# Mixing and 16-head attention of a four-block decoder as one program block on one Trainium2 core

## The chip, the cores and the metric

The kernel runs on one core of one Trainium2 chip. The metric is the device time of one execution in microseconds; the kernel before was run three times (1469.81, 1473.39 and 1476.22 us, median 1473.39). One further execution was recorded by the hardware profiler; that one took 1470.31 us, of which 1468.5 us lie between its first and its last instruction. The instruction queues are called by their engines: TensorE (PE, with its weight loads PEld), VectorE (DVE), ScalarE (ACT), GpSimd (POOL) and SyncE (SP, which issues the DMAs).

## The reference

The input x has 32 sequences of 128 tokens with 128 features (float32). Four layers alternate cross attention against a context (128 tokens, 96 features) and a feed-forward part, each added to x. What matters here is the end of layer 1 and the start of layer 2:

- layer 1's block takes the result of its first attention, modulated, adds a state-space convolution, runs a multilayer part `gelu(LN(z) W1 + b1) W2 + b2`, normalises and adds it to x;
- layer 1's feed-forward part picks one of 8 experts **per sequence**: each expert's small autoencoder (128 to 32 and back) tries to reconstruct the normalised tokens, the expert with the least error wins, and its down and up matrices (128 to 64 to 128, with relu) are added to a shared product with W_base, gated;
- layer 2's attention has 16 heads of 8 features: q from LN(x), k and v from the context, softmax over the 128 context tokens, an output matrix Wo with bias, gated and added to x. Layer 2's feed-forward part quantises LN(x) with one scale for the whole tensor, so it needs the largest absolute value of all of it.

## The kernel before, in words

X stays in on-chip memory (`k.X`, 128 partitions of tokens, 32 sequences). The stages run one after the other, each a block of programs for the five queues, with a barrier and a clearing of its semaphores behind it (class OneTime, the clear and barrier are reported at L72): `stage_front`, `stage_film`, `stage_mix` (L1679), `stage_attention16` (L2096), `stage_last`. The two in the middle are the ones touched.

**stage_mix** works on groups of four sequences (8 groups) in a software pipeline, loop variable n from -1 to 10, written out by hand in the same order for all queues. In step n group n goes through the multilayer part (L1857, L1828, L1902), group n-1 is normalised, added to X and normalised again to `xa` (L2013, third use), group n-2 goes through the reconstruction (transposes of xa L1862, L1832, L1843, L1845, the squares L2066, the loss L2069, the four small products L1922 to L1925, then the gain and the choice `at`, L2089 to L2093), and for group n-3 SyncE loads the four chosen numbers into registers (L1758) and issues four DMAs for the down matrices (L1765) and four for the up matrices (L1770); TensorE waits for them and does the down products (L1888), ScalarE the relu (L1994), TensorE the output products (L1913, L1915), VectorE adds them to X (L2084). In TensorE's queue the output products of group n-3 stand before the small sums of group n-2. Steps 8, 9 and 10 are the last three: there is no multilayer part left in them, and in step 10 only the last group's expert. GpSimd computes reciprocal square roots (L1783, L1785) and some sums of whole groups; its last work is in step 8.

**stage_attention16** prepares constants (GpSimd: zeroes v, top, sel, L2169 to L2173; VectorE: mod32, hmask, nsel, bo, L2335 to L2345, with one product on TensorE, L2204) and then runs a pipeline over n from -7 to 37. Steps below 0 open it: for group 0 statistics (L97), moments (L178 to L188), rstd (L2179), application (L195), then one item per step on PSUM bank 7, k (L2275), x transposed (L2279), q (L2283) and v (L2286), each evacuated by ScalarE. GpSimd adds the bias to X (L2189) and masks q for the four bands of heads (L2197). From then on each n is a sequence: scores (L2219), peak of each row (L2351), its transpose (L2258), scores transposed with the peak subtracted (L2231, L2235), exp (L2299), product with v (L2249) and sums (L2253), reciprocal, Wo (L2266), sum into X (L2399). The next group's k, x, q and v are made one per step beside it. The scores of sequence 0 belong to step n = -1. The last stage begins with the largest value (L2724).

The waits are counters; each queue runs its instructions in the order in which they are written, so an instruction that waits holds up all behind it in its queue.

Of the kernel before, what the change touches and what calls it, by code (L numbers as in the profile page):

```python
# [5 lines left out]
F32 = mybir.dt.float32  # L6
# [1672 lines left out]
def stage_mix(nc, w, ps, k):  # L1679
# [5 lines left out]
    GROUPS = B // G  # L1685
    with ExitStack() as ctx:
# [3 lines left out]
        fo, u_ = tmp("fo", [128, 2, G, 256]), tmp("u", [128, 3, G, 128])  # L1690
        z, last = tmp("z", [128, 3, G, 128]), tmp("last", [128, G, 128])
        nmr = tmp("nmr", [128, B])
        xn, hT = tmp("xn", [128, G, 128]), tmp("hT", [128, W])
        hid = tmp("hid", [128, 4, W])
# [3 lines left out]
        xa, xaT = tmp("xa", [128, G, 128]), tmp("xaT", [128, 2, W])  # L1698
# [24 lines left out]
        ve1_done, ve2_done, ve3_done = (once(n) for n in ("ve1_done", "ve2_done", "ve3_done"))  # L1723
        block = ctx.enter_context(nc.Block())
# [17 lines left out]
        def flat(ap):  # L1742
            return ap.rearrange("p j d -> p (j d)")

# [68 lines left out]

        @block.tensor
        def _(pe):
# [34 lines left out]

            for n in range(FIRST, LAST):
# [26 lines left out]
                if has(n - 2):  # L1878
                    recon(n - 2, 1)
                if has(n - 3):  # L1880
# [24 lines left out]
                if has(n - 3):  # L1905
# [10 lines left out]
                    m.then_inc(out_ps, 1)  # L1916
                if has(n - 2):
# [7 lines left out]
                    pe.matmul(o, k.ones[:, 0:G], k.bd2q[:], start=False, stop=True).then_inc(sum_ps, 1)  # L1925

        @block.scalar
        def _(act):
# [30 lines left out]

            plain(0)  # L1960
            for n in range(FIRST, LAST):
# [24 lines left out]
                if has(n + 2):  # L1986
                    plain(n + 2)
                if has(n - 3):
# [4 lines left out]
                    for j in range(G):  # L1993
                        act.activation(aT[0:R, j, :], ps[0:R, 0, j * S:j * S + S], ACT.Relu,  # L1994
                                       bias=dn[0:R, g % 2, j, R:R + 1]).then_inc(aT_done, 1)

        @block.vector
        def _(dve):
# [11 lines left out]
            def apply(dst, src, mv, rs, rs_done, done, g):  # L2010
                dve.wait_ge(rs_done, g + 1)
                for j in range(G):
                    dve.tensor_scalar(dst[:, j, :], src[:, j, :], mv[:, j, 0:1], rs[:, j:j + 1], ALU.subtract,  # L2013
                                      ALU.mult).then_inc(done, 1)

            for n in range(FIRST, LAST):
# [69 lines left out]
                if has(n - 2):  # L2086
# [6 lines left out]
                    dve.max_index(at[:], best[:], gain[:]).then_inc(at_done, 1)  # L2093


def stage_attention16(nc, w, ps, k):  # L2096

    H, DH = 16, 8
    SCALE = DH ** -0.5
    R = 4
    GROUPS = B // G
    with ExitStack() as ctx:
        def tmp(name, shape, dt=F32):
            return ctx.enter_context(nc.sbuf_tensor("g_" + name, shape, dt))

        nm = Norm(lambda n, s: ctx.enter_context(nc.sbuf_tensor(n, s, F32)), "g")  # L2110
        on = Norm(lambda n, s: ctx.enter_context(nc.sbuf_tensor(n, s, F32)), "go")
        xall = k.x3[:].rearrange("p a b -> p (a b)").rearrange("p (b c) -> p b c", b=B)
        xn, xnT = tmp("xn", [128, 2, G, 128]), tmp("xnT", [128, W])
        qT, kT = tmp("qT", [128, 2, W]), tmp("kT", [128, 2, W])
        mod32, hmask = tmp("mod32", [128, 32]), tmp("hmask", [128, R])
        nsel = tmp("nsel", [128, R, 128])
        mq = tmp("mq", [128, 3, R, 128])
        v, sel = tmp("v", [128, 2, G, R, 160]), tmp("sel", [128, 160])
# [992 lines left out]
```

## Time and profile before

| | |
|---|---|
| runs, median (lowest to highest) | 1473.39 us (1469.81 to 1476.22) |
| profiled execution, its span | 1470.31 us, 1468.5 us |
| instructions | 30801 |
| TensorE busy, mean granted clock | 1182.5 us (81%), 0.862 |
| VectorE, ScalarE, GpSimd busy | 997.4, 689.2, 545.7 us |
| mixing, 16-head attention (first to last instruction) | 492.4 to 695.9, 697.0 to 938.7 us |

Times in a timeline are microseconds from the first instruction. A row of it is a run of like instructions on one queue: start, length from the first start to the last end, engine, line, operation, tiles written and read, shape, count; in brackets the idle time of the engine in front of it and what ended that. [...]

### The profile page before, as it was taken

Reading aid. Unit: us, or ns where it says so; the run is one execution under the profiler, and the core shown is the slowest. Engines: PE = TensorE matmul, PEld = TensorE weight load, DVE = VectorE, ACT = ScalarE, POOL = GpSimd, SP = SyncE. Lnnn points to the kernel's source line nnn. Section 1 sums busy time; section 2 is a strip of 40 time slices with the busy share of each in tenths; the row PEclk is TensorE's granted clock in tenths of the full one; section 3 lists DMA queues with packets and bytes.
Section 4 is the critical chain, followed back from the end, with each engine's and each line's share of the span. In section 5 each row is a group of like instructions: output and inputs, shape, how many; then the busy total and the mean of one; then the engine's idle time right before and its main releaser. Section 6 shows DMA issues by size and latency. Waiting matters only on the chain. (4 is left out here: it accounts for less than half of the span.)

```text
span 1468.5 us, 30801 instructions
## 1 busy us (share of the span) xinstructions
PE 1182.5 (81%) x10551; PEld 809.7 (55%) x10551; DVE 997.4 (68%) x3895; ACT 689.2 (47%) x2022; POOL 545.7 (37%) x769
## 2 busy tenths in 40 slices
PE   4767764667766678885699988589999989999998
PEld 3533322434444455553477777356666657777766
DVE  6767759999996478851577776677776654544443
ACT  3343336777764334321244544347666653433333
POOL 4576565777664255520322231244333320000000
PEclk7779775776766699995799999789999999998989
DMA  6301031010002411000000000000000000000000
GB/s 167 95 1 33 12 99 47 16 30 19 26 23 73 122 29 44 16 15 15 2 3 3 3 3 3 1 1 1 2 1 1 2 1 1 15 0 14 0 15 15
DMA packets 63745, 35.59 MB, mean 24 GB/s; under 512 B 23989, under 2 KB 61488, under 8 KB 63602
## 3 DMA queue, kind: packets, MB, share of 16 engines
q1 hardware_dynamic: 62298, 33.45, 8.3%
q8 instruction: 79, 1.29, 0.4%
q14 instruction: 64, 0.52, 0.1%
q10 hardware_dynamic: 1304, 0.33, 0.1%
HBM read 25.21 MB, written 6.42 MB: 22 GB/s over the span
## 5 line engine op out<-in xcount | busy, mean ns | idle before, releaser
L2994 DVE SCALAR_TENSOR_TENSOR k_X<-ps,m_gt,k_X 128x128 f32 (+1 forms) x256 | 72.2, 345 | 120.9 <-PE ps L2878 120.8
L2917 ACT ACTIVATE m_hid<-ps,k_b 128x512 f32<-128x512 f32 x128 | 81.8, 684 | 133.2 <-PE ps L2878 127.7
L2878 PEld LDWEIGHTS ps<-k_w,m_hid 128*128 128x128 f32 x1024 | 123.1, 192 | 26.8 <-issue 19.6
L2867 PE MATMUL ps<-m_xnT,k_w 128*128 128x512 f32 x256 | 128.2, 631 | 1.3 <-PEq L72 1.3
L2878 PE MATMUL ps<-k_w,m_hid 128*128 128x128 f32 x1024 | 123.4, 275 | 0.0
L2538 POOL TENSOR_TENSOR l_p<-l_p,l_rsum 128x512 f32<-128x512 f32 x64 | 65.2, 1039 | 139.2 <-DVE l_rsum L2816 139.2
L2351 DVE TENSOR_REDUCE g_top<-ps 128x8 f32<-128x1024 f32 x64 | 75.4, 1220 | 50.4 <-PE ps L2219 50.4
L1587 DVE MATCH_REPLACE8 v_left<-c_top,v_left 128x128 f32<-128x128 f32 x384 | 107.2, 410 | 0.0
L2299 ACT ACTIVATE g_pT<-ps 128x1024 f32<-128x1024 f32 x64 | 62.0, 1021 | 85.3 <-PE ps L2235 85.3
L2670 ACT ACTIVATE l_p<-ps,l_shift 128x128 f32<-128x128 f32 x256 | 91.4, 389 | 21.2 <-DVE l_shift L2757 19.9
L711 PE MATMUL ps<-f_expT,f_xeT 128*128 128x512 f32 x128 | 73.3, 705 | 27.4 <-DVE k_X L1089 27.3
L1581 DVE MAX8 c_top<-v_left 128x8 f32<-128x128 f32 x384 | 84.0, 403 | 0.0
L1587 DVE MATCH_VALUE_LOAD v_left<-c_top,v_left 128x8 f32 x384 | 73.7, 214 | 0.0
L121 POOL TENSOR_TENSOR m_rstd<-m_ve,k_half 128x8 f32<-128x8 f32 x4 | 6.6, 1639 | 175.0 <-DVE m_ve L114 175.0
L2867 PEld LDWEIGHTS ps<-m_xnT,k_w 128*128 128x128 f32 x256 | 47.8, 205 | 41.2 <-issue 41.2
L842 ACT ACTIVATE f_part<-ps,f_wf 128x128 f32<-128x128 f32 x128 | 36.4, 368 | 72.6 <-issue 47.0
L1389 PE MATMUL ps<-k_ident,c_exa 128*128 128x128 f32 x256 | 56.4, 411 | 10.4 <-POOL c_exa L1334 10.4
L1389 PEld LDWEIGHTS ps<-k_ident,c_exa 128*128 128x128 f32 x256 | 53.9, 318 | 18.3 <-POOL c_exa L1334 18.1
L711 PEld LDWEIGHTS ps<-f_expT,f_xeT 128*128 128x128 f32 x128 | 25.5, 223 | 65.9 <-DVE k_X L1089 44.9
L2670 ACT ACTIVATION_READ_ACCUMULATOR l_p<-ps,l_shift 128x1 f32 x256 | 58.8, 230 | 0.0
L1089 DVE SCALAR_TENSOR_TENSOR k_X<-ps,f_wf,k_X 128x128 f32<-128x128 f32 x128 | 44.6, 349 | 20.3 <-PE ps L711 16.3
L1373 PE MATMUL ps<-c_kT,c_qT 32*128 32x128 f32 x256 | 21.7, 419 | 45.3 <-ACT v_sc L1468 42.6
(537 smaller groups left out, 3178.2 us busy)
## 6 DMA issues: line engine op xcount, KB each, us to landing
v_toep<-kpad SPq DMA_DIRECT2D x4, 1024.0 KB, 9.3
fo_dram<-c_fo SPq DMA_DIRECT2D x32, 128.0 KB
d_fo<-fo_dram SPq DMA_DIRECT2D x8, 512.0 KB, 3.6
k_X<-in_x SPq DMA_DIRECT2D x8, 256.0 KB, 3.5
v_late<-kpad SPq DMA_DIRECT2D x2, 1024.0 KB, 8.4
out<-k_X SPq DMA_DIRECT2D x8, 256.0 KB, 2.4
f_cx<-in_ctx SPq DMA_DIRECT2D x4, 384.0 KB, 5.5
c_cx<-in_ctx SPq DMA_DIRECT2D x4, 384.0 KB, 4.3
```

Of the source, the lines that this page charges most:

```text
L711: pe.matmul(ps[:, 4 + (2 * b + h) % 3, :], xeT[:, t % 2, u, cols], expT[:, 4 * h:4 * h + 4, :].rearrange("p e d -> p (e d)"), start=True, ...
L1389: m = pe.matmul(ps[:, 4 + a, 0:128], exa[:, i % 4, h, :], k.ident[:], start=h == 0, stop=h == H - 1)
L1581: dve.max((first if r == 0 else top)[:, a, h, :], (sc if r == 0 else left)[:, i % 4, h, :]).then_inc(top_done, 1)
L1587: dve.match_replace(left[:, i % 4, h, :], (first if r == 0 else top)[:, a, h, :], (sc if r == 0 else left)[:, i % 4, h, :], TAKEN).then_in ...
L2299: act.activation(pT[:, n % 2, 2 * h:2 * h + 2, :].rearrange("p a n -> p (a n)"), ps[:, 4 + 2 * h:6 + 2 * h, :].rearrange("p a n -> p (a n) ...
L2351: dve.tensor_reduce(top[:, (n + 1) % 2, :].rearrange("p (r c) -> p r c", r=R)[:, 2 * h:2 * h + 2, 0:R], ps[:, 2 * h:2 * h + 2, :].rearrang ...
L2538: pool.tensor_tensor(p[:, n % 3, 4 * a:4 * a + 4, :], p[:, n % 3, 4 * a:4 * a + 4, :], rsum[:, n % 3, 4 * a:4 * a + 4].rearrange("p (h o) ...
L2670: act.activation(p[:, i % 3, h, :], ps[:, 2 * (i % 2) + a, 128 * b:128 * b + 128], ACT.Exp, bias=shift[:, i % 2, h:h + 1], scale=SCALE, ac ...
L2867: pe.matmul(ps[:, 4 * u + q, :], k.w1_3[:, e, 128 * q:128 * q + 128], xnT[:, u], start=True, stop=True).then_inc(s["hid_ps"].sem, 1)
L2878: m = pe.matmul(ps[:, 4 * u + 2 + e % 2, j * S:j * S + S], hid[:, u, q, j * S:j * S + S], k.w2_3[:, e, q, :], start=q == 0, stop=q == 1)
L2917: act.activation(hid[:, u, q, :], ps[:, 4 * u + q, :], ACT.Gelu, bias=k.b1_3[:, 2 * e + q:2 * e + q + 1]).then_inc(s["hid"].sem, 1)
L2994: dve.scalar_tensor_tensor(out=xj[u][j], in0=ps[:, 4 * u + 2 + e % 2, j * S:j * S + S], scalar=gt[:, u, j, e:e + 1], in1=xj[u][j], op0=ALU ...
```

## The change

The two stages become one, `stage_mix_attend`, with one block. The attention's step becomes a function `attend(n)` on each queue, called with the old bodies. Names that clashed are renamed (xn to an, xnT to anT, top to peak, topT to peakT, out_ps to ao_ps, x_done to sum_done, R to BANDS). The bias product goes to PSUM bank 2 instead of 0. Eight of the mixing's tiles no longer have memory of their own: they are parts of the attention's v and pT, so that zeroing v waits until the last multilayer product is made and the last z begun.

Where the opening steps are called now, in the mixing's last three steps (GROUPS is 8, so GROUPS + 1 is step 9). The memory:

```diff
+        v, pT = keep("v", [128, 2, G, BANDS, 160]), keep("pT", [128, 2, BANDS, W])
+        low = v[:].rearrange("p u j a x -> p (u j a x)")
+        fo = low[:, 0:2048].rearrange("p (u j c) -> p u j c", u=2, j=G)
+        hid = low[:, 2048:4096].rearrange("p (q n) -> p q n", q=4)
+        xn = low[:, 4096:4608].rearrange("p (j d) -> p j d", j=G)
+        hT = low[:, 4608:5120]
+        low = pT[:].rearrange("p u a n -> p (u a n)")
+        u_ = low[:, 0:1536].rearrange("p (u j d) -> p u j d", u=3, j=G)
+        z = low[:, 1536:3072].rearrange("p (u j d) -> p u j d", u=3, j=G)
+        last = low[:, 3072:3584].rearrange("p (j d) -> p j d", j=G)
+        xa = low[:, 3584:4096].rearrange("p (j d) -> p j d", j=G)
```

GpSimd, behind the mixing's whole loop:

```diff
+            pool.wait_ge(mlp_ps, GROUPS)
+            pool.wait_ge(zs, GROUPS)
+            pool.memset(v[:], 0.0).then_inc(zeroed, 1)
+            pool.memset(peak[:], 0.0).then_inc(zeroed, 1)
+            pool.memset(sel[:], 0.0).then_inc(zeroed, 1)
+            pool.wait_ge(zeroed, 3)
+            pool.memset(sel[:].rearrange("p (b x) -> p b x", x=40)[:, :, 0:DH], 1.0).then_inc(sel_done, 1)
...
+            for n in range(OPEN, CLOSE):
+                attend(n)
```

TensorE, in the mixing's loop and behind it:

```diff
                 if has(n - 2):
                     recon(n - 2, 1)
+                if n == GROUPS + 1:
+                    pe.matmul(ps[:, 2, 0:128], k.bv2[:].broadcast_to([128, 128]), k.wo2[:], start=True,
+                              stop=True).then_inc(bvo_ps, 1)
+                    pe.wait_ge(left, GROUPS)
+                    attend(-5)
+                if n == GROUPS + 2:
+                    attend(-2)
                 if has(n - 3):
                     g = n - 3
...
                     m.then_inc(out_ps, 1)
+                if n == GROUPS + 1:
+                    attend(-4)
                 if has(n - 2):
...
                     pe.matmul(o, k.ones[:, 0:G], k.bd2q[:], start=False, stop=True).then_inc(sum_ps, 1)
+                if n == GROUPS + 1:
+                    attend(-3)
+
+            pe.wait_ge(bo_sum, 1)
+            pe.wait_ge(sel_done, 1)
+            pe.wait_ge(nsel_done, 1)
+            attend(-1)
+
+            pe.wait_ge(gain_done, GROUPS)
+            pe.wait_ge(xo_done, GROUPS)
+            for n in range(0, CLOSE):
+                attend(n)
```

ScalarE:

```diff
                 if has(n + 2):
                     plain(n + 2)
+                if n == GROUPS + 1:
+                    attend(-5)
+                if n == GROUPS + 2:
+                    act.wait_ge(zeroed, 3)
+                    attend(-3)
+                    attend(-2)
                 if has(n - 3):
...
+                if n == GROUPS + 1:
+                    attend(-4)
+
+            for n in range(-1, CLOSE):
+                attend(n)
```

VectorE (the four places are behind sx, behind the loss, behind xa and at the end of the step):

```diff
                     dve.tensor_reduce(sx[:], xaT[:, g % 2, :].rearrange("p (j t) -> p j t", j=G), AX.X,
                                       ALU.add).then_inc(sx_done, 1)
+                if n == GROUPS + 1:
+                    attend(-5)
...
+                if n == GROUPS + 1:
+                    dve.tensor_reduce(mod32[:], k.ident[:].rearrange("p (r c) -> p c r", r=BANDS), AX.X,
+                                      ALU.add).then_inc(mod_done, 1)
+                    dve.wait_ge(mod_done, 1)
+                    dve.tensor_reduce(hmask[:], mod32[:].rearrange("p (b d) -> p b d", b=BANDS), AX.X,
+                                      ALU.add).then_inc(hmask_done, 1)
+                    dve.wait_ge(bvo_ps, 1)
+                    dve.tensor_tensor(bo[:], ps[:, 2, 0:128], k.bo2[:], ALU.add).then_inc(bo_sum, 1)
+                    dve.wait_ge(bo_sum, 1)
+                    dve.tensor_scalar(bo[:], bo[:], k.tg[:, 2:3], None, ALU.mult).then_inc(bo_done, 1)
...
                     apply(xa, group(k.X, g), mv3, rs3, rs3_done, xa_done, g)
+                if n == GROUPS:
+                    attend(-7)
+                    attend(-6)
...
                     dve.max_index(at[:], best[:], gain[:]).then_inc(at_done, 1)
+                if n == GROUPS + 1:
+                    dve.tensor_scalar(nsel[:], mod32[:, 0:BANDS].rearrange("p (b o) -> p b o", o=1).broadcast_to([128, BANDS, 128]),
+                                      -1.0, None, ALU.mult).then_inc(nsel_done, 1)
+                    dve.wait_ge(zeroed, 3)
+                    attend(-3)
+                    attend(-2)
+
+            for n in range(-1, CLOSE):
+                attend(n)
```

And the list of stages:

```diff
-        stages = [stage_front, stage_film, stage_mix, stage_attention16, stage_last]
+        stages = [stage_front, stage_film, stage_mix_attend, stage_last]
```

What `attend` does at the steps named: on VectorE -7 the statistics and -6 the moments of group 0, -5 its application to `an`, -3 and -2 statistics and moments of group 1, -1 the peaks of sequence 0; on TensorE and ScalarE -5 k, -4 x, -3 q, -2 v of group 0, -1 the scores of sequence 0 and k of group 1. On GpSimd -6 is rstd of group 0, -4 the bias into X of group 0, -2 rstd of group 1 and then the masked q of sequence 0, -1 that of sequence 1.

## Rows read from the trace of the kernel before

**Rows 1.** The page: span of the profiled execution.
```profile
span 1468.5 us, 30801 instructions
```

**Rows 2.** Busy by stretch: us, PE, PEld, DVE, ACT, POOL, granted clock, DMA, GB/s.
```profile
661.40:678.00 16.60, 13.54 (x54) 8.24 (x50) 4.64 (x10) 3.09 (x7) 0.00 (x0) 0.71 0.07 17
678.00:697.00 19.00, 5.92 (x30) 5.17 (x26) 1.81 (x7) 1.12 (x4) 0.04 (x1) 0.50 0.06 14
697.00:714.90 17.90, 9.89 (x50) 5.72 (x50) 9.83 (x31) 2.57 (x4) 10.46 (x9) 0.51 0.01 1
```

**Rows 3.** Timeline, the mixing's last step (10).
```profile
678.98 0.15 DVE L2093 FIND_INDEX8 d_at<-d_best,d_gain 4x8 uint32<-4x8 f32 x1
...
689.32 1.94 PE L1888 MATMUL ps<-d_xaT,d_dn 128*64 128x128 f32 x8 [11.21 <-DMA d_up<-k_wup]
...
694.49 0.63 PE L1915 MATMUL ps<-d_up,d_aT 65*128 65x128 f32 x2
695.16 0.75 DVE L2084 SCALAR_TENSOR_TENSOR k_X<-ps,k_tg,k_X 128x512 f32<-128x512 f32 x1 [16.04 <-PE ps L1915]
```

**Rows 4.** Timeline, the attention's opening up to the first peak.
```profile
696.96 4.36 POOL L2169 MEMSET g_v<- 128x5120 f32 x1 [41.44 <-POOLq L72]
...
697.51 4.10 DVE L2340 TENSOR_SCALAR g_nsel<-g_mod 128x512 f32<-128x512 f32 x1
...
702.05 0.87 DVE L97 BATCH_NORM_STATS2 g_stats<-k_X 128x6 f32<-128x128 f32 x4
702.08 0.12 POOL L2173 MEMSET g_sel<- 128x32 f32 x1
...
702.30 2.04 PE L2275 MATMUL ps<-k_cT,k_wk 96*128 96x512 f32 x2 [4.54 <-POOL g_sel L2173]
...
703.71 0.17 DVE L188 TENSOR_SCALAR g_ve<-g_m 128x4 f32<-128x4 f32 x1
...
706.26 1.09 PE L2279 MATMUL ps<-k_ident,g_xn 128*128 128x128 f32 x4 [1.91 <-DVE g_xn L195]
...
712.95 1.95 PE L2219 MATMUL ps<-g_kT,g_mq 32*128 32x128 f32 x32
...
714.97 2.35 DVE L2351 TENSOR_REDUCE g_top<-ps 128x8 f32<-128x1024 f32 x2 [6.75 <-PE ps L2219]
```

**Rows 5.** Timeline, end of the mixing's step 8 on GpSimd and VectorE.
```profile
654.48 1.04 POOL L1785 TENSOR_TENSOR d_rs<-d_rs,k_half 128x4 f32<-128x4 f32 x1
...
656.55 1.11 DVE L2013 TENSOR_SCALAR d_xa<-k_X,d_mv,d_rs 128x128 f32<-128x128 f32 x4
...
661.31 0.75 DVE L2084 SCALAR_TENSOR_TENSOR k_X<-ps,k_tg,k_X 128x512 f32<-128x512 f32 x1 [3.65 <-PE ps L1915]
...
662.42 0.15 DVE L2093 FIND_INDEX8 d_at<-d_best,d_gain 4x8 uint32<-4x8 f32 x1
```

**Rows 6.** Timeline, the mixing's step 9.
```profile
661.48 1.12 PE L1862 MATMUL ps<-k_ident,d_xa 128*128 128x128 f32 x4
...
672.82 1.15 PE L1888 MATMUL ps<-d_xaT,d_dn 128*64 128x128 f32 x8 [2.37 <-DMA d_up<-k_wup]
...
677.92 0.20 PE L1925 MATMUL ps<-k_bd2q,k_ones 128*4 128x8 f32 x2
678.54 0.14 DVE L2089 TENSOR_SCALAR d_gain<-ps 4x8 f32<-4x8 f32 x1
```

**Rows 7.** First VectorE instruction behind the seam into mixing and into attention.
```profile
492.48 0.19 DVE L1999 TENSOR_TENSOR d_nmr<-k_mv,k_rstd 128x32 f32<-128x32 f32 x1 [1.16 <-PEq L72]
...
697.00 0.37 DVE L2335 TENSOR_REDUCE g_mod<-k_ident 128x32 f32<-128x128 f32 x1 [1.08 <-PEq L72]
```

**Rows 8.** Timeline, one output product of step 7.
```profile
642.76 0.39 PE L1915 MATMUL ps<-d_up,d_aT 65*128 65x128 f32 x2
```

**Rows 9.** Timeline, scores of the third and the fourth sequence.
```profile
725.37 1.17 PE L2219 MATMUL ps<-g_kT,g_mq 32*128 32x128 f32 x32 [0.52 <-ACT g_topT L2304]
...
731.67 1.17 PE L2219 MATMUL ps<-g_kT,g_mq 32*128 32x128 f32 x32 [0.38 <-DVE g_oT L2394]
```

More of the change, by code:

```diff
@@ L1676, in _, with stage_mix_attend @@
                 dve.tensor_copy(chunk(c), ps[:, c, :])
-def stage_mix(nc, w, ps, k):
+def stage_mix_attend(nc, w, ps, k):
     R, E = 64, 8
     GROUPS = B // G
+    H, DH = 16, 8
+    SCALE = DH ** -0.5
+    BANDS = 4
     with ExitStack() as ctx:
@@ new lines, in stage_mix_attend @@
+        nsel = keep("nsel", [128, BANDS, 128])
+        mq = keep("mq", [128, 3, BANDS, 128])
+        sel = keep("sel", [128, 160])
+        peak, peakT = keep("peak", [128, 2, 128]), keep("peakT", [128, 2, 128])
+        rsum, oT = keep("rsum", [128, 128]), keep("oT", [128, 2, 128])
+        bo = keep("bo", [128, 128])
+        each = ctx.enter_context(OneTime(nc, "g_"))
+        zeroed, sel_done, mod_done, hmask_done, nsel_done, bvo_ps, bo_sum, bo_done = (
+            each(n) for n in ("zeroed", "sel_done", "mod_done", "hmask_done", "nsel_done", "bvo_ps", "bo_sum",
+                              "bo_done"))
@@ new lines, in stage_mix_attend @@
+        stats, halves, square, mean, ve, rstd, an_done, xb = (
+            each(n) for n in ("stats", "halves", "square", "mean", "ve", "rstd", "an_done", "xb"))
+        o_stats, o_halves, o_square, o_mean, o_ve, o_rstd, o_shift, o_done, most_done = (
+            each(n) for n in ("o_stats", "o_halves", "o_square", "o_mean", "o_ve", "o_rstd", "o_shift", "o_done",
+                              "most_done"))
+        onorm = dict(stats=Signal(o_stats, 0, 2 * G, k.apart), halves=Signal(o_halves, 0, 6, k.apart),
+                     square=Signal(o_square, 0, 4, k.apart), mean=Signal(o_mean, 0, 2, k.apart),
+                     ve=Signal(o_ve, 0, 2, k.apart))
@@ new lines, in stage_mix_attend @@
+        k_ps, kT_done, xT_ps, xT_done, q_ps, qT_done, v_ps, v_done = (
+            each(n) for n in ("k_ps", "kT_done", "xT_ps", "xT_done", "q_ps", "qT_done", "v_ps", "v_done"))
+        mq_done, sc_ps, top_done, topT_ps, topT_done, st_ps, ex_done, av_ps, rsum_done, oT_done, ao_ps, sum_done = (
+            each(n) for n in ("mq_done", "sc_ps", "top_done", "topT_ps", "topT_done", "st_ps", "ex_done", "av_ps",
+                              "rsum_done", "oT_done", "ao_ps", "sum_done"))
+        norm = dict(stats=Signal(stats, 0, 2 * G, k.apart), halves=Signal(halves, 0, 6, k.apart),
+                    square=Signal(square, 0, 4, k.apart), mean=Signal(mean, 0, 2, k.apart),
+                    ve=Signal(ve, 0, 2, k.apart), rstd=Signal(rstd, 0, 2, k.apart),
+                    xn=Signal(an_done, 0, 2 * G, k.apart))
@@ L1743, in flat, with item, evacuated, batch @@
             return ap.rearrange("p j d -> p (j d)")
+        OPEN, CLOSE = -7, B + 6
+        def item(n):
+            g, what = (n + 5) // G, ("k", "x", "q", "v")[(n + 5) % G]
+            return (what, g) if n >= -5 and g < GROUPS else (None, g)
+        def evacuated(eng, n):
+            what, g = item(n)
+            if what == "k":
+                eng.wait_ge(kT_done, g + 1)
+            elif what == "x":
+                eng.wait_ge(xT_done, g + 1)
+            elif what == "q":
+                eng.wait_ge(qT_done, g + 1)
+            elif what == "v":
+                eng.wait_ge(v_done, g + 1)
+        def batch(n):
+            return (n // G) % 2, slice((n % G) * S, (n % G) * S + S)
         @block.sync
```

499 lines of the change are left out of this document (207 added, 292 removed).

## The prediction

> **What bounds the kernel now.** I first read the page for the whole [rows 1]: 1468.5 us of span inside a profiled execution of 1470.31 us, which is 3.08 us under the median of the three runs (1473.39). [...]
>
> The timeline gives the chains. Last mixing step [rows 3]: the expert is chosen at 679.1, SyncE loads the four numbers and issues eight DMAs, TensorE waits 11.21 us and starts L1888 only at 689.32 when the last `up` has landed, then the output matmuls to 695.12 and the sum into X at 695.16. All engines are nearly free from 679 to 689. Opening of the attention [rows 4]: a barrier, a memset of v (4.36 us), then statistics, transposes, q, v, masked q, and at 712.95 the first scores; the first peak reduction starts at 714.97. From L2204 to 712.95 nothing is overlapped with mixing. What is moved ends in front of the scores, and all that follows them waits for them, so the number to find is when the scores of batch 0 start.
>
> **The change, part by part.**
>
> *Removed from the seam.* Scores start at 712.95, the last L1915 of mixing ends at 694.49 + 0.63 = 695.12 [rows 3, 4]. In the changed order of TensorE nothing stands between the two but waits for constants, v and masked q. If these are long done, scores follow at once: **-17.8 us** (712.95 - 695.12). The barrier is in it.
>
> *Are they done?* What is left after the step-9 sums (steps are numbered as the loop's n; 8, 9, 10 are the last three) is in the trace the way from the transposes L2279 (706.26) to the scores (712.95), 6.7 us [rows 4], at the low clock too. It starts at about 678 and so ends near 685, plus 2 to 3 us for nsel and the statistics of group 1, behind which POOL's masking waits: 688 at the latest, against TensorE's own 695. Cover: the 11.21 us of DMA wait. Some 7 us to spare, so I cost all of k, x, q, v, masking, nsel at nothing. Without that cover it would be the 6.7.
>
> *The memsets, step 8.* They sit behind POOL's last mixing work, which ends at 654.48 + 1.04 = 655.52 [rows 5]. In the trace they last from 696.96 to 702.20, 5.24 us [rows 4], so to about 660.8. VectorE wants to start `xa` (L2013, four tensor_scalar, 1.11 us) at 656.55 [rows 5], inside the big memset. The row for that: nsel, a tensor_scalar begun at 697.51 beside the same memset, took 4.10 us and ended 0.3 after it [rows 4], where four of a quarter of its size take 1.11 [rows 5]. So xa ends near 655.55 + 4.36 + 1.11 = 661.0 instead of 657.66. The transposes of xa start at 661.48 anyway [rows 6]: free. But behind xa the change puts the statistics and moments of group 0, 702.05 to 703.88 = 1.83 us [rows 4], to 662.9; the sum into X, due at 661.31 [rows 5], is 1.6 late, and the choice of expert at 662.57 with it. From there the chain (SyncE, DMA, L1888) runs without slack. **+1.6.** Bounds: 0, if the memset doesn't block (3.65 us of idle time before 661.31 take 1.83), and 3.0 if each small memset also stops one of the four. I take the middle one, as the row is of the same pair of instructions. [...]
>
> *Step 9.* The k matmul and the bias product go into TensorE's wait for the DMA, the gap before L1888, 2.37 us in this step [rows 6] and 1.6 longer with the delay above; k takes 2.04 at the low clock [rows 4], the other is a quarter as wide: free. On VectorE the application for group 0 (1.1) comes before the work that waits for L1845, and the constants (1.2) after the loss, both well ahead of the sum into X and the gain at 678.54 [rows 6]. The transposes of x do fall in the chain: they stand between the output matmuls and the four sums. They cost 1.12 at low clock, by the four at L1862 of the same form [rows 6]. The sums end at 677.92 + 0.20 = 678.12, the gain is taken at 678.54 [rows 6], so 0.4 is free: **+0.7** (0.2 if the clock is high; at most 1.1).
>
> *Step 10.* On SyncE's queue nothing is added. ScalarE's evacuations of q and v stand in front of aT, VectorE's nsel, statistics and moments in front of the sum into X; both have the DMA wait as cover. 0.
>
> *The end.* Two sets of semaphores are now cleared together at the end of the attention, where one was cleared at each seam. The seam with one set shows 1.08 us of idle time, the seam into mixing, which clears two, 1.16 [rows 7]. **+0.1** (up to 1.1, a whole seam).
>
> *Shared memory.* The waits that guard it (last multilayer product, last z) are long past where they are used, and the mixing loop keeps its own waits: 0. Steps 0 to 7 should be unchanged.
>
> Sum: -17.8 + 1.6 + 0.7 + 0.1 = **-15.4 us**. Against the profiled execution 1470.3 - 15.4 = 1454.9; against the median 1473.39 - 15.4 = **1458.0**, which I give.
>
> **Rivals.**
>
> *A, the delays don't come (gain 17 to 19.5).* The memset blocks nothing (+1.6 more), the transposes hide (+0.7), and TensorE's clock stays high in step 9: at 642.76 the two passes of a product at L1915 take 0.39 us, at low clock 0.63 [rows 3, 8]; over the eight products of the output phase that is 1.9 us. For it: the idle time before L1888 in step 9 is partly filled. Against: 1.6 us of new idle time. [...] Time 1454 to 1456.
>
> *B, the chain takes more (gain 10 to 13).* If all added VectorE and TensorE work of steps 8 and 9 falls into the chain of choosing: 3.0 + 1.1 + 1.2 + 1.1 instead of 2.3, 4.1 less: 1462. For it: that chain has no slack. Against: the idle times named.
>
> *C, the preparation isn't ready (gain 5 to 9).* One of its eight hand-overs waits behind a mixing instruction until after the DMA, and the rest, up to 6.7, follows it: 1464.7. Against it: each is issued before the dn matmuls.
>
> [...]
>
> **How the numbers follow.** Forecast 0.55; A 0.24, B 0.11, C 0.05, D 0.03, and 0.02 that the seam hides something that gives back most of it. 0.5% is 7.4 us, about what a measurement of this kernel can tell from no change. Forecast, A and B are faster by more (0.90), and so is a part of C: 0.92; the rest of C and the hidden thing: 0.05; D: 0.03. Range: from A's best with the lowest run before (1469.8 - 19 = 1451) to B's with some spread above, 1464.
>
> **What would show it.** In the changed profile: memset of v from about 655.5, the xa group at some 4 us instead of 1.11, the sum into X of step 8 at 663; choice of step 9 1.6 us, L1888 of step 10 about 2.3 us later than 689.32; scores of batch 0 right after the last L1915, near 697.4; first peak reduction near 699.4 instead of 714.97; the same 6.3 us per batch; one seam of about 1.2 us in front of the last stage. Wrong would be: scores that wait for a masked q or v, mixing steps 0 to 7 of another length, or a granted clock under 1.0 past the third batch.

## The result and the profile after

The changed kernel took **1456.38 us** (median of five runs, 1452.09 to 1462.50), the kernel before beside it 1473.39 us (five runs, 1469.81 to 1476.22): a ratio of 0.9888, 95% interval [0.9856, 0.9919], so 17.0 us less. The range (1451 to 1464) held it, and the forecast of 1458.0 was 1.6 us too high. The same kernel, run again unedited, gave 1457.35 us against 1472.81 (ratio 0.9893 [0.9876, 0.9910], 15.5 us less).

The execution that was profiled is the fastest of its five. The page's first line, to set beside [rows 1]:

```profile
span 1450.3 us, 30794 instructions
```

18.2 us less than before, but not all of it is the change's. The timeline at the start of mixing, whose code is the old one:

```profile
487.64 0.19 DVE L2266 TENSOR_TENSOR d_nmr<-k_mv,k_rstd 128x32 f32<-128x32 f32 x1 [1.16 <-PEq L72]
```

In [rows 7] it stands at 492.48; when the changed kernel was run again, unedited, it stood at 494.36. The stages ahead of mixing vary by 6.7 us between executions of the same instructions, so I compare profiles from this instruction on: to the first reduction of the last stage it is 447.23 us before (939.71 - 492.48) and 433.71 after (921.35 - 487.64), **13.5 us less**.

**Step 8.** The timeline of GpSimd and VectorE, which answers [rows 5]:

```profile
650.79 4.37 POOL L1891 MEMSET g_v<- 128x5120 f32 x1
651.86 4.36 DVE L2280 TENSOR_SCALAR g_pT<-k_X,d_mv,d_rs 128x128 f32<-128x128 f32 x4
...
656.15 0.63 PE L2117 MATMUL ps<-d_up,d_aT 65*128 65x128 f32 x2
...
657.85 0.74 DVE L2422 SCALAR_TENSOR_TENSOR k_X<-ps,k_tg,k_X 128x512 f32<-128x512 f32 x1
...
658.96 0.15 DVE L2431 FIND_INDEX8 d_at<-d_best,d_gain 4x8 uint32<-4x8 f32 x1
```

`xa` (its tile is now part of pT) takes 4.36 us instead of 1.11: one of its four pieces alone is shown as 3.79 us long, and the memset beside it ends at 655.16. The last output product ends at 656.78 and the sum into X starts 1.07 us behind it, where it started 0.04 behind before (660.64 + 0.63 against 661.31). The choice is 1.03 late.

**Step 9**, the timeline of all engines, which answers [rows 6]:

```profile
665.82 1.02 PE L2030 MATMUL ps<-k_cT,k_wk 96*128 96x512 f32 x2
...
669.35 1.94 PE L2090 MATMUL ps<-d_xaT,d_dn 128*64 128x128 f32 x8 [2.50 <-DMA d_up<-k_wup]
...
674.52 0.63 PE L2117 MATMUL ps<-d_up,d_aT 65*128 65x128 f32 x2
...
674.95 0.92 PE L2034 MATMUL ps<-k_ident,g_an 128*128 128x128 f32 x4
...
676.18 0.15 DVE L2427 TENSOR_SCALAR d_gain<-ps 4x8 f32<-4x8 f32 x1 [0.24 <-PE ps L2129]
...
676.64 0.15 DVE L2431 FIND_INDEX8 d_at<-d_best,d_gain 4x8 uint32<-4x8 f32 x1
```

k (one float32 product, which its row counts as x2; in front of it the bias product, 0.39) lies in the wait for the DMA. The transposes of x (L2034) stand between outputs and sums: the gain comes 1.03 behind the last output product (675.15), before 0.71 (677.83 to 678.54). From the first down product to the end of the outputs it is 5.80 us, before 5.01: the down products took 1.94 us at a granted clock of 0.50, before 1.15 at 0.86. I call 0.50 the lower level and 1.00 the high one: the first scores of this profile, below, took 2.09 us at 0.50 and the third 1.17 at 1.00.

**The preparation, step 10 and the seam that is gone** (timeline, answering [rows 3, 4]):

```profile
676.65 1.10 PE L2038 MATMUL ps<-g_anT,k_wq 128*128 128x512 f32 x2 [0.50 <-ACT g_anT L2196]
...
679.91 2.04 POOL L1919 TENSOR_TENSOR g_mq<-g_qT,g_hmask 128x512 f32<-128x512 f32 x2
680.34 0.60 ACT L2206 ACTIVATE g_v<-ps 128x512 f32<-128x512 f32 x1 [1.81 <-PE ps L2041]
...
686.97 1.94 PE L2090 MATMUL ps<-d_xaT,d_dn 128*64 128x128 f32 x8 [6.67 <-DMA d_up<-k_wup]
...
692.14 0.64 PE L2117 MATMUL ps<-d_up,d_aT 65*128 65x128 f32 x2
692.71 2.09 PE L1974 MATMUL ps<-g_kT,g_mq 32*128 32x128 f32 x32
692.82 0.75 DVE L2422 SCALAR_TENSOR_TENSOR k_X<-ps,k_tg,k_X 128x512 f32<-128x512 f32 x1 [13.98 <-PE ps L2117]
694.87 2.36 DVE L2287 TENSOR_REDUCE g_peak<-ps 128x8 f32<-128x1024 f32 x2 [1.30 <-PE ps L1974]
...
699.39 2.09 PE L1974 MATMUL ps<-g_kT,g_mq 32*128 32x128 f32 x32
...
706.33 1.17 PE L1974 MATMUL ps<-g_kT,g_mq 32*128 32x128 f32 x32 [0.52 <-ACT g_peakT L2187]
```

All of group 0 is ready at 681.95, 10.8 us before the scores, and these follow the last output product at once. From the choice to the down products it is 10.33 us, before 10.34. The third scores are at the high level (1.17 us, 1.00), as they were, and the fourth start 6.30 us behind them (712.63), as in [rows 9].

**The end.** The first row of the last stage, first of the kernel before (not shown above), then of the changed kernel:

```profile
939.71 0.16 DVE L2724 TENSOR_REDUCE l_amax<-k_most 128x1 f32<-128x8 f32 x1 [1.03 <-PEq L72]
```

```profile
921.35 0.16 DVE L2764 TENSOR_REDUCE l_amax<-k_most 128x1 f32<-128x8 f32 x1 [1.78 <-PEq L72]
```

0.75 us more for two clearings in a row.

### The profile page after: what moved, and what is told of

Read it like the earlier page. It is cut to its first block and busy times, and to the rows that moved or that the text cites. A ratio compares the mean times of both kernels' runs of the same rounds, so it can differ in the third digit from the quotient of the medians.

```text
span 1450.3 us, 30794 instructions
## 1 busy us (share of the span) xinstructions
PE 1175.4 (81%) x10551; PEld 805.8 (56%) x10551; DVE 995.7 (69%) x3895; ACT 689.0 (48%) x2022; POOL 545.8 (38%) x769
## 5 line engine op out<-in xcount | busy, mean ns | idle before, releaser
L2287 DVE TENSOR_REDUCE g_peak<-ps 128x8 f32<-128x1024 f32 x64 | 75.4, 1219 | 45.8 <-PE ps L1974 45.8
L1587 DVE MATCH_REPLACE8 v_left<-c_top,v_left 128x128 f32<-128x128 f32 x384 | 100.8, 274 | 0.0
L1581 DVE MAX8 c_top<-v_left 128x8 f32<-128x128 f32 x384 | 77.8, 274 | 0.0
L1389 PE MATMUL ps<-k_ident,c_exa 128*128 128x128 f32 x256 | 55.9, 407 | 10.3 <-POOL c_exa L1334 10.2
L1389 PEld LDWEIGHTS ps<-k_ident,c_exa 128*128 128x128 f32 x256 | 53.5, 316 | 18.1 <-POOL c_exa L1334 17.9
L1452 ACT ACTIVATE c_exb<-v_left,c_shift 128x128 f32<-128x128 f32 x128 | 49.6, 391 | 12.9 <-DVE v_left L1587 12.9
```

Source lines behind the costliest of these rows:

```text
L1389: m = pe.matmul(ps[:, 4 + a, 0:128], exa[:, i % 4, h, :], k.ident[:], start=h == 0, stop=h == H - 1)
L1581: dve.max((first if r == 0 else top)[:, a, h, :], (sc if r == 0 else left)[:, i % 4, h, :]).then_inc(top_done, 1)
L1587: dve.match_replace(left[:, i % 4, h, :], (first if r == 0 else top)[:, a, h, :], (sc if r == 0 else left)[:, i % 4, h, :], TAKEN).then_in ...
L2287: dve.tensor_reduce(peak[:, (n + 1) % 2, :].rearrange("p (r c) -> p r c", r=BANDS)[:, 2 * h:2 * h + 2, 0:BANDS], ps[:, 2 * h:2 * h + 2, :] ...
```

## The experiments

All kernels compute the reference, and each ran beside the kernel before, to which its ratio refers. The kernels of a group below ran on one chip; there the kernel before took 1472.81 us in the first group, 1472.78 in the second and 1471.52 in the third.

### First group: is it the overlap, and are the terms there?

**The changed kernel again, no edit.** 

> The changed kernel once more, unedited. In its first profile mixing began 4.8 us earlier than before, though nothing in front of it is changed. Theory 1 (that is a difference from execution to execution, TensorE's clock in the first stage): the start of mixing comes anywhere within some 5 us of 492.5, and what the change itself does, from the first instruction of mixing to the end, is -13.4 us again, as in the first profile. Theory 2 (the change does it, by the way code or tiles lie): the start of mixing is near 487.6 again and in every variant, and the whole is 17 to 18 us faster.

Measured: 1457.35 us (1454.69 to 1458.71). As far as the rows show, its profile differs from the first in TensorE's clock alone. Timeline:

```profile
677.39 1.06 PE L2090 MATMUL ps<-d_xaT,d_dn 128*64 128x128 f32 x8 [1.28 <-DMA d_up<-k_wup]
...
697.11 1.17 PE L1974 MATMUL ps<-g_kT,g_mq 32*128 32x128 f32 x32
...
701.88 1.17 PE L1974 MATMUL ps<-g_kT,g_mq 32*128 32x128 f32 x32
```

Down products of step 9 at 1.06 instead of 1.94, first and second scores at 1.17 instead of 2.09, all three at a granted clock of 1.00, in the first profile 0.50. From the start of mixing to the last stage it took 427.90 us at a mean granted clock of 0.94 (first profile 0.91), **5.8 less than the first profile of the same instructions**, and 19.3 less than the kernel before. So of theory 1 the first half came true (mixing began at 494.36) and the second did not: the -13.4 us of the first profile is not a fixed number. One profile can't give the change's worth to better than some 6 us, and terms of 0.3 to 1 us have to be read locally, as the distance between two neighbouring instructions.

**The opening steps behind mixing again**, still one block with shared memory and no barrier:

```diff
+            pool.wait_ge(xo_done, GROUPS)      # in front of the memsets
...
-                if n == GROUPS + 1:
...
-                    attend(-5)
...
+            for n in range(-5, -1):            # TensorE, behind the loop
+                attend(n)
...
+            for n in range(OPEN, CLOSE):       # ScalarE and VectorE
+                attend(n)
```

> One block and shared memory as in the change, but memsets, constants and the opening steps of the attention stand behind the mixing's last sum into X again; only the barrier between the stages is gone. Theory 1 (the gain is the overlap): the seam from the last L1915 to the first scores is some 17 us again (17.83 before, less a barrier of 1), steps 8 and 9 get back their old pace, the end keeps its second clearing: -1 to 0 us against before, some 13 us slower than the change. Rival (the gain is the barrier and the merged block): over half of the gain stays, under 1465 us.

Measured: 1471.14 us (1468.19 to 1473.40, twelve runs), ratio 0.9987 [0.9976, 0.9997]. Timeline around its seam:

```profile
692.16 1.94 PE L2083 MATMUL ps<-d_xaT,d_dn 128*64 128x128 f32 x8 [11.22 <-DMA d_up<-k_wup]
...
714.90 2.09 PE L1975 MATMUL ps<-g_kT,g_mq 32*128 32x128 f32 x32
```

The sum into X is at 698.00, so the scores come 16.9 us behind it, before 17.8 (695.16 to 712.95). Taking the barrier out brings 0.9 here, which the second clearing (1.78 us in front of the last stage, as after the change) nearly gives back. The kernel is 1.7 us faster than the one before, a little more than my -1 to 0; the move of the opening work into mixing is nearly the whole gain.

**The sums in front of the transposes of x** in step 9:

```diff
@@ TensorE, step 9
-                if n == GROUPS + 1:
-                    attend(-4)
...
                     pe.matmul(o, k.ones[:, 0:G], k.bd2q[:], start=False, stop=True).then_inc(sum_ps, 1)
                 if n == GROUPS + 1:
+                    attend(-4)
                     attend(-3)
```

> In step 9 TensorE makes the four sums before the transposes of x instead of behind them. Theory: the transposes stand in the chain sums, choice, DMA; the time from the last output matmul to the gain goes from 1.03 us back to 0.70: -0.3 us, nothing that the medians can tell; the profile must show it. Rival: they cost nothing, as the sum into X hides them: the distance stays 1.03.

Measured: 1458.03 us (1455.78 to 1459.21). Timeline:

```profile
681.55 0.63 PE L2117 MATMUL ps<-d_up,d_aT 65*128 65x128 f32 x2
...
682.89 0.14 DVE L2426 TENSOR_SCALAR d_gain<-ps 4x8 f32<-4x8 f32 x1
```

The gain is 0.71 behind the last output product (682.18) again, against 1.03 after the change: the transposes' term is 0.32 us. In the time of the whole it can't be seen.

**The memsets behind xa.** One wait, so that the memset of v begins when xa is done:

```diff
             pool.wait_ge(zs, GROUPS)
+            pool.wait_ge(xa_done, G * GROUPS)
             pool.memset(v[:], 0.0).then_inc(zeroed, 1)
```

> GpSimd waits until xa of the last group is made before it zeroes v. Theory (the memset keeps VectorE's tensor_scalar group waiting): xa takes 1.1 us instead of 4.36 and the sum into X of step 8 comes at the end of the output matmuls instead of 1.0 us behind it: -1.0 us at most. Rival (the group is slow for another reason, its place in the shared tile or the work order): xa still takes over 4 us.

Measured: 1457.25 us (1456.98 to 1457.53). A gain of 1 us could hardly be told from these times; the rows show that it didn't come. Timeline:

```profile
657.42 1.11 DVE L2281 TENSOR_SCALAR g_pT<-k_X,d_mv,d_rs 128x128 f32<-128x128 f32 x4
...
658.67 4.36 POOL L1892 MEMSET g_v<- 128x5120 f32 x1 [2.28 <-DVE g_pT L2281]
...
659.76 3.29 DVE L183 TENSOR_SCALAR g_mean<-g_mean 128x4 f32<-128x4 f32 x1
...
663.19 0.74 DVE L2423 SCALAR_TENSOR_TENSOR k_X<-ps,k_tg,k_X 128x512 f32<-128x512 f32 x1
```

xa is done before the memset begins and takes 1.11. But the memset now holds a tensor_scalar over 128x4 numbers, 3.29 us instead of 0.16, and the sum into X behind it starts 6.80 us behind the end of the mixing's last rstd on GpSimd (656.39), after the change 7.01 (650.84 to 657.85). The block went to the next tensor_scalar, small as it is: L183 starts 1.09 us behind the memset and ends at 663.05, the memset at 663.03.

### Second group: where are the rest and a better order?

**All semaphores of the block in one set**, so one clearing and one barrier at its end:

```diff
-        each = ctx.enter_context(OneTime(nc, "g_"))
+        def each(name):
+            return once("g_" + name)
```

> All semaphores of the merged block belong to one set, cleared once behind it. Theory (the second clearing and its barrier stand at the end): the idle time in front of the first instruction of the last stage goes from 1.78 us back to about 1.05: -0.7 us, 1456.6. Rival (the longer seam comes from the number of semaphores, not from the number of barriers): it stays at 1.78.

Measured: 1454.91 us (1451.18 to 1460.21, six runs). Timeline:

```profile
926.80 0.16 DVE L2766 TENSOR_REDUCE l_amax<-k_most 128x1 f32<-128x8 f32 x1 [1.41 <-PEq L72]
```

1.41 us: half-way between 1.03 and 1.78. So 0.37 of the 0.75 belong to the second clearing and barrier. The other 0.38 stay with one set, which has more semaphores in it: 100, where the attention's own had 45 (counted in the kernels' code). No run varies their number alone, but the rows of before fit this reading. The seam into the attention clears one set of 55 and shows 1.08; the seam into mixing clears two sets with only 13 in all and shows 1.16 [rows 7]. From 45 at 1.03 and 100 at 1.41 I estimate 0.007 us for each semaphore; with 0.37 for a second clearing that gives 1.18 for the seam into mixing.

**TensorE kept busy in the waits for the DMA**, with 4, 2 and 6 constant products in steps 8, 9 and 10 whose result nobody reads:

```diff
+                    if not has(n):
+                        for _ in range((4, 2, 6)[n - GROUPS]):
+                            pe.matmul(ps[:, 3, :], k.ident[:], k.w1_1[:], start=True, stop=True)
                     pe.wait_ge(chosen_in[g % 2], 16 * 2 * G * (g // 2 + 1))
```

> [...] Theory (the granted clock, which falls in those waits, decides the length of the output phases and of the first two scores, and is what differs between executions of one kernel): the down and output products take 3.4 us instead of 5.8 in each step and the first scores 1.17 instead of 2.09: -7 us, about 1450, and a smaller spread between executions. Rival (the clock is not governed by these waits, or the added work delays the down products by as much): 1457 or more.

Measured: 1454.63 us (1453.37 to 1455.59), from mixing to the last stage 430.26. Timeline:

```profile
660.48 1.09 PE L2093 MATMUL ps<-d_xaT,d_dn 128*64 128x128 f32 x8 [1.05 <-DMA d_up<-k_wup]
...
667.13 3.78 PE L1945 MATMUL ps<-d_xaT,k_wd 128*128 128x512 f32 x4 [0.69 <-ACT d_xaT L2233]
...
678.51 1.09 PE L2093 MATMUL ps<-d_xaT,d_dn 128*64 128x128 f32 x8 [0.47 <-DMA d_up<-k_wup]
...
693.40 1.09 PE L2093 MATMUL ps<-d_xaT,d_dn 128*64 128x128 f32 x8 [2.00 <-DMA d_up<-k_wup]
```

All three down products run at the high level (1.09 us, 1.00). The 4, 2 and 6 constant products took 3.60, 1.88 and 5.32 us, at 1.00 too. The runs lie within 2.2 us, against 10.4 in the first five and 4.0 in the second set of the unedited kernel, but that isn't shown to come from the added products: with the memsets behind xa and none of these products, four runs lie within 0.6. In step 8 the faster outputs (the last ends at 663.91) bring nothing. The sum into X waits for VectorE's blocked run and starts at 667.10, 7.03 us behind the last rstd (660.07), as in both unedited profiles (7.01 and 7.02). TensorE waits 1.32 us for xa, and L1945 behind it is at the low level, 3.78 us at 0.50, as it was in the second unedited profile. The expected 7 us didn't come: the time is 18.2 us under the kernel before, where the unedited kernel was 17.0 and 15.5 under it, and by the ratio (0.9873 [0.9853, 0.9892]) the two can't be told apart.

**Choose before the output products.** In steps 8 and 9 the sums and the choice of group n-2 go in front of the down products of n-3, on TensorE and VectorE; the tile `at` is doubled, as SyncE may still be reading the old choice:

```diff
-        gain, best, at = tmp("gain", [G, 8]), tmp("best", [G, 8]), tmp("at", [G, 8], U32)
+        gain, best, at = tmp("gain", [G, 8]), tmp("best", [G, 8]), tmp("at", [G, 2, 8], U32)
...
+                if has(n - 2) and not has(n):
+                    sums(n - 2)               # TensorE, in front of the wait for the DMA
...
+                if has(n - 2) and not has(n):
+                    choose(n - 2)             # VectorE, in front of the sum into X
```

> In steps 8 and 9 the four sums and the choice of the expert come before the output phase of the group before, on TensorE and on VectorE (the index tile doubled). Theory (the last steps are bound by the chain choice, DMA, output, sums, choice): each choice comes some 5 us earlier against its step and the whole is 4 to 6 us faster, about 1452. Rival (what binds is the DMA's own time, or TensorE's order of work): under 2 us.

Measured: **1447.88 us** (1444.25 to 1451.08), ratio 0.9833 [0.9813, 0.9854]. Timeline:

```profile
655.93 0.15 DVE L2349 FIND_INDEX8 d_at<-d_best,d_gain 4x8 uint32<-4x8 f32 x1
...
662.58 1.98 PE L1945 MATMUL ps<-d_xaT,k_wd 128*128 128x512 f32 x4 [0.69 <-ACT d_xaT L2234]
...
671.03 0.15 DVE L2349 FIND_INDEX8 d_at<-d_best,d_gain 4x8 uint32<-4x8 f32 x1
...
681.34 1.24 PE L2101 MATMUL ps<-d_xaT,d_dn 128*64 128x128 f32 x8 [3.14 <-DMA d_up<-k_wup]
```

The last choice comes 180.3 us behind the start of mixing (490.70), in the first profile of the changed kernel 189.0; to the last stage it is 424.16 us. In step 9 the down products start at 670.46 right behind the sums, with no wait for the DMA left. The chain that bounded the last steps was this one: choice, registers and DMA (10.3 us), down, output, next choice. Between the choices of steps 8 and 9 it binds no more: what stands there now (15.10 us) is the outputs of step 8, the transposes of xa, the reconstruction and its loss. The gain was more than I expected. How much of the 9.5 us between the two profiles is the clock again (the down products of step 9 took 1.09 us at 1.00, not 1.94 at 0.50) the ratios tell better: 0.9833 against 0.9888 and 0.9893, 8 to 9 us, with some 4 us to either side by their intervals.

**The memsets behind GpSimd's rstd of group 0**, which comes behind xa, the statistics and the moments of VectorE:

```diff
-            pool.memset(v[:], 0.0).then_inc(zeroed, 1)
...
+            attend(-7)
+            attend(-6)
...
+            pool.memset(v[:], 0.0).then_inc(zeroed, 1)
```

> The memsets stand behind GpSimd's rstd of group 0, so that no tensor_scalar of step 8 runs beside them (behind xa alone they held up the one of the moments, 3.29 us). Theory: the sum into X of step 8 comes at once behind its output products, the choice 1.0 us earlier; what is held up now is the application of group 0, some 4 us, with 9 us until it is needed: -1.0 us. Rival: the held-up application pushes squares, loss and sums of step 9 and gives it back: 0 or slower.

Measured: 1454.04 us (1452.14 to 1455.93). Timeline:

```profile
658.54 1.11 DVE L2282 TENSOR_SCALAR g_pT<-k_X,d_mv,d_rs 128x128 f32<-128x128 f32 x4
...
662.40 4.37 POOL L1920 MEMSET g_v<- 128x5120 f32 x1
662.77 0.75 DVE L2424 SCALAR_TENSOR_TENSOR k_X<-ps,k_tg,k_X 128x512 f32<-128x512 f32 x1 [1.40 <-PE ps L2119]
...
664.87 2.98 DVE L195 TENSOR_SCALAR g_an<-k_X,g_mean,g_rstd 128x128 f32<-128x128 f32 x4
```

Now the sum into X waits only for the outputs (they end at 662.74) and isn't late, although the memset began 0.37 us before it. The block falls on the application for group 0, which has time. The step-8 term is gone locally; the ratio, 0.9871 [0.9851, 0.9891], overlaps that of the unedited kernel, which it must for a term of 1 us.

### Third group: the edits together

**Early choice, one set, and the memsets behind GpSimd's bias sum.** The edits of above, with the memsets moved down to between `attend(-4)` and `attend(-3)` of GpSimd.

> Three edits together: sums and choice in front of the output products of the group before (as in the kernel that chooses early), all semaphores of the new block in one set, and the memsets of v, peak and sel moved on GpSimd's queue behind its sum of the bias into X, so to about 672 us, where VectorE has only work for the attention's preparation and one sum into X. Theory, the terms add: against the early choice alone (1447.88, from the start of mixing to the last stage's first reduction 424.16) the block on xa of 3.21 us instead of 1.11 is not in the chain any more there, since the output products on TensorE end later than it (0), and the second clearing's half goes (-0.4): about 423.8 and a median of 1447.5. Rival: the memset at 672 holds the sum into X of step 9 or nsel and the statistics by up to 4 us, and the masked q comes after the last output product: a wait of POOL in front of the scores, 0.5 to 3 us more. Second rival: the freed xa starts the chain of the last choice earlier, 1 to 2 us less.

Measured: **1447.81 us** (1447.00 to 1449.70), ratio 0.9835 [0.9820, 0.9851], as the early choice alone. Timeline:

```profile
664.41 3.78 PE L1949 MATMUL ps<-d_xaT,k_wd 128*128 128x512 f32 x4 [0.69 <-ACT d_xaT L2238]
...
675.54 0.15 DVE L2353 FIND_INDEX8 d_at<-d_best,d_gain 4x8 uint32<-4x8 f32 x1
...
678.06 4.36 POOL L1922 MEMSET g_v<- 128x5120 f32 x1
678.45 0.75 DVE L2440 SCALAR_TENSOR_TENSOR k_X<-ps,k_tg,k_X 128x512 f32<-128x512 f32 x1 [1.74 <-PE ps L2132]
679.11 4.01 DVE L2445 TENSOR_SCALAR g_nsel<-g_mod 128x512 f32<-128x512 f32 x1
```

The median is the forecast one, but the profile isn't: from mixing to the last stage it took 427.28 us, where I expected 423.8. Between the choices of steps 8 and 9 lie 17.94 us (657.60 to 675.54), in the early choice alone 15.10. The block on xa isn't the reason, as xa takes 1.09 us here; the first reconstruction products (L1949) ran at the low level, 3.78 us at 0.50 where those of the early choice took 1.98 at 1.00. Again the clock hides what a single profile is asked for.

nsel is held 4.01 us, as [rows 4] has it. The masked q is done at 687.95, 3.7 us before the scores (691.61), so the wait of the first rival isn't there. But a smaller form of it is, in ScalarE's queue:

```profile
682.87 0.69 ACT L2209 ACTIVATE g_qT<-ps,k_bq 128x512 f32<-128x512 f32 x1 [3.39 <-POOL g_sel L1924]
```

ScalarE waits for all memsets in front of its evacuation of q, not only in front of that of v. So TensorE waits too (2.89 us) and makes v at the lower level, 2.08 us at 0.50. The last down products still start 10.34 us behind the choice, at 685.88, but take 1.94 us (0.50) instead of 1.24 (0.80); that the wait cost them the level is my reading. These 0.7 us are more than the 0.37 that the single set gives (its seam is 1.41 again), and neither can be seen in the medians.

**The same with TensorE kept busy**: three constant products in front of the sums of step 8, three in front of the last wait for the DMA, and the second group's k in front of the wait for the first peak.

```diff
+                    if n == GROUPS:
+                        for _ in range(3):
+                            pe.matmul(ps[:, 3, :], k.ident[:], k.w1_1[:], start=True, stop=True)
                     sums(n - 2)
...
+                    if n == GROUPS + 2:
+                        for _ in range(3):
+                            pe.matmul(ps[:, 3, :], k.ident[:], k.w1_1[:], start=True, stop=True)
                     pe.wait_ge(chosen_in[g % 2], 16 * 2 * G * (g // 2 + 1))
...
+                if n == -1:
+                    evacuated(pe, n - 1)
+                    pe.matmul(ps[:, 7, :], k.wk2[:], k.cT[:, W:2 * W], start=True, stop=True).then_inc(k_ps, 1)
```

> The kernel with the three edits, with TensorE kept busy besides: three constant products in front of the sums of step 8 and three in front of the down products of step 10, both in waits that TensorE has anyway (5.32 and 3.14 us), and the second group's k product put in front of the wait for the first peak instead of behind it. No output changes. Theory, TensorE's clock in these steps is what differs between executions: down and output products of steps 8 and 10 at 1.09 and about 3.4 us, the first scores at 1.17 instead of 2.09, the second scores 1 to 2 us earlier: 4 to 6 us less than the three edits alone in executions where those were at the low level, so a median about 3 us lower, and a smaller spread between the lowest and highest run. Rival: the clock is not held by work put just in front (the products themselves run at the low level, 1.9 us each, and end after the wait they fill): no gain, or 1 to 2 us more.

Measured: 1450.50 us (1446.83 to 1451.42), ratio 0.9854 [0.9837, 0.9871]: no gain that can be told, and the runs lie within 4.6 us, no closer than without it (2.7). Timeline:

```profile
673.28 0.15 DVE L2362 FIND_INDEX8 d_at<-d_best,d_gain 4x8 uint32<-4x8 f32 x1
...
683.49 4.85 PE L2111 MATMUL ps<-k_w,k_ident 128*128 128x512 f32 x6
688.27 1.09 PE L2114 MATMUL ps<-d_xaT,d_dn 128*64 128x128 f32 x8
...
691.62 1.17 PE L1987 MATMUL ps<-g_kT,g_mq 32*128 32x128 f32 x32
...
696.06 1.17 PE L1987 MATMUL ps<-g_kT,g_mq 32*128 32x128 f32 x32 [0.46 <-ACT g_peakT L2204]
```

The gap that the three products of step 10 were meant for (3.14 us with the early choice alone) was closed by then: v was late, for the reason just shown. They ran at a mean of 0.56 and took 4.85 us, so the down products, due at 673.28 + 10.3 = 683.6, began 4.7 late. Behind them the down products (1.09 us) and the first and second scores (1.17 each) are at the high level, 1.00, the second scores 4.4 us behind the first instead of 6.7 (4.8 in the second unedited profile, where k hadn't been moved), which gives about as much back: from the last choice to the third scores it is 28.0 us, without the added products 29.1. The rival came true, though partly by my placing. From choice to choice this kernel took 15.07 us with xa free, the early choice 15.10 with xa blocked (3.21 us at 656.01), both with the first reconstruction products at the high level (1.98 us, 1.00): with that order the block isn't in the chain, and the second rival of the three edits falls.

## Why the prediction was right, by its own steps

The sum was -15.4 us; the medians moved by 17.0 and 15.5 us in the two comparisons. Against the first profile, from mixing on, -13.5.

- **Seam, -17.8: right.** Scores were 17.83 behind the last output product and are now 0.07 before its modelled end, -17.9. The room for it is in [rows 2], where TensorE is busy less than a third of the last step. The cause is shown: with the opening put back behind mixing, and still no barrier between, all but 1.7 us of the gain is gone.
- **Preparation at nothing: right, and with more to spare.** I put its end at "688 at the latest" and it was 681.95 in a profile that began mixing 4.8 us earlier, so 686.8 by the old scale, and 10.8 us were left where I counted 7. Rival C had nothing to stand on.
- **Step 8, +1.6: mechanism right, size too large.** It measured 1.03 at the choice. xa ended 5.38 us behind the mixing's last rstd, where I had 5.5; statistics and moments took 1.81 us but overlapped xa and the sum by 0.2, and the outputs themselves came 0.2 later. Freeing xa alone (memsets behind xa) removes hardly anything, while memsets behind the moments of group 0 remove the whole delay. That shows both halves: it is the memset, and it held not xa alone (4.36 us instead of 1.11) but, with xa done, the small L183 (3.29 instead of 0.16) in the run of VectorE work in front of the sum. What I didn't see is that the term has no fixed size. The sum into X starts when both the outputs and VectorE's run are done, and the run's end is steady, 7.01, 7.02 and 7.03 us behind the last rstd in three profiles. What it costs is what the outputs leave of it: in the second unedited profile the sum starts 0.72 behind them, in the first 1.07, with TensorE kept busy 3.19.
- **Step 9, +0.7: size too large, 0.32.** I took 1.12 for the four transposes, the length of such a row at the low level (0.50 there), and 0.4 of slack. Theirs is 0.92 long at 0.65, between that and the 0.60 of the second profile, at 1.00, and the tail of the last one overlaps what follows: the sums begin 1.28 us behind the start of the last output product (674.52 to 675.80), before 0.56 (677.20 to 677.76), so the transposes cost them 0.72. With the slack of 0.4, which was as I read it, 0.32 is left. The second unedited profile shows the case of the high level, which I had put at 0.2: the gain comes 0.75 behind the last output product (680.79 to 681.54), before 0.71, so 0.04.
- **The end, +0.1: this step failed.** I read the seams of [rows 7], 1.16 for two sets against 1.08 for one, as the price of a second set. It cost 0.75: the seam into the last stage was 1.03 and became 1.78, and with one set 1.41. The upper bound I kept (1.1) held. Two seams that clear different sets are not a measurement of the second clearing: the two sets in front of mixing have 13 semaphores together, the one in front of the attention 55, and by the estimate above that hid 0.3 of the 0.37.
- **The clock, which the sum left out.** In the first profile step 9 lost 0.8 us to it (5.80 us at 0.50, before 5.01 at 0.58) and the first three scores another 1.2 (13.62 us from the first to the third at 0.63, before 12.42 at 0.80). With these, -17.9 + 1.03 + 0.32 + 0.75 + 0.8 + 1.2 = -13.8, against -13.5 measured; most of the rest is 0.2 in steps 0 to 7 and 0.2 in the outputs of step 8. In the second profile of the same kernel the clock went the other way and it is -19.3 from mixing on. So rival A had a piece of the truth: its high clock in step 9 is what some executions have (1.06 us for the down products there, 1.00). Others have the low level at the second scores (2.09 us at 0.50), and so had the kernel before (2.09 too), but in every profile the third took 1.17. The 0.03 of D was for a kernel slower than before, and none was measured.

The forecast was near for a reason that was partly luck: terms of 1.6, 0.7 and 0.1 that measured 1.03, 0.32 and 0.75 nearly make the same sum (2.4 forecast, 2.1 measured). And that the median lay within 1.6 us says little of terms of this size: two sets of runs of the changed kernel gave 17.0 and 15.5 us less, and the clock, alone as far as the rows show, moved one profile by 5.8.

## What to carry to other kernels

Independent opening work of a next stage is worth its whole exposed length if it fits into a wait that the previous stage has anyway; find the latest such wait and count the time to spare. When what is left is a chain through a choice and a DMA, move the choice ahead of work that doesn't need it: here that brought another 8 to 9 us by reordering alone. Don't put a long memset on GpSimd where VectorE has a tensor_scalar in front of work that is waited for (here one of 128x4 took 3.29 us instead of 0.16), and compare small terms between neighbouring instructions, not between profiles.

## What the runs showed of the hardware that I had not expected

- A memset of 128x5120 held a tensor_scalar over 128x4 numbers for 3.29 us (0.16 alone), but the sum into X, a scalar_tensor_tensor over 128x512 with one operand in PSUM, took its usual 0.75 in two kernels (at 662.77 and at 678.45), although it began inside the memset both times. A tensor_scalar over 4x8 numbers in PSUM, the gain at 663.44, took 0.14 inside the first of them.
- The seams fit a cost that goes with the number of semaphores cleared there, as well as with the number of clearings, though no run varies the first alone: 1.03 us for one set of 45, 1.08 for one of 55, 1.41 for one of 100, 1.78 for two sets of 100 together, but 1.16 for two sets of 13 together.
- The same instructions took 433.71 and 427.90 us over the same stretch in two executions, at a mean granted clock of 0.91 and 0.94; as far as the rows show, nothing else differs. The stages ahead of mixing differed by 6.7 us (487.64 at 0.76, 494.36 at 0.74). In the middle of a kernel too, behind the same 0.69 us of waiting, the first reconstruction products took 3.78 us at 0.50 with the three edits and 1.98 at 1.00 with the early choice alone.
- Work put in front of a product didn't always raise its level in time: three constant products took 4.85 us at 0.56 from 683.49 on, behind 3.2 us of waiting and v at the low level, where three in step 8 of the same kernel took 2.74 at 1.00, and behind those, after 2.76 us of waiting, the down products were at the low level again (1.97 at 0.50).
